# The order of TensorE's steps in a fused attention and feed-forward layer: from the first candidate in a priority, to the one with the earliest due time

## The reference

```python
qkv = x @ W_qkv.T
q, k, v = jnp.split(qkv, 3, axis=-1)
scores = jnp.einsum('bhqd,bhkd->bhqk', q, k) / math.sqrt(D_HEAD)
scores = jnp.where(mask, scores, -jnp.inf)
attn = jax.nn.softmax(scores, axis=-1)
out = jnp.einsum('bhqk,bhkd->bhqd', attn, v)
return out @ W_proj.T
...
x = _layernorm(x + _L0_attn_ref(x, L0_attn_W_qkv, L0_attn_W_proj), axis=-1)
x = _layernorm(x + _L0_ffn_ref(x, L0_ffn_w_gate, L0_ffn_w_up, L0_ffn_w_down), axis=-1)
```

## Time and profile before

| | |
|---|---|
| median of three runs | 1428.83 us (1426.91 to 1429.59) |
| profiled execution, its own time | 1426.97 us |
| its span, first to last instruction | 1425.3 us |
| busy: TensorE, VectorE, ScalarE, GpSimd | 95%, 78%, 62%, 24% of the span |
| mean granted TensorE clock | 0.984 of full |

### The profile page before, as it was taken

One profiled execution on the slowest core, in us unless ns is written; L12 is line 12 of the kernel. 1 busy time (PEld: TensorE's weight loads), 2 busy tenths in 40 slices (PEclk: granted clock), 3 DMA queues, 4 the chain that ended last, 5 costly groups with the idle time before them and its releaser, 6 DMA issues.

```text
span 1425.3 us, 29068 instructions
## 1 busy us (share of the span) xinstructions
PE 1353.2 (95%) x11348; PEld 661.3 (46%) x11348; DVE 1106.7 (78%) x1649; ACT 890.7 (62%) x1985; POOL 345.4 (24%) x448
## 2 busy tenths in 40 slices
PE   7999988999999999999999999999979999999997
PEld 4666643333333333333333333333336666666664
DVE  4455468988889888889888889888625877878876
ACT  2333335787787787787888788778763443444433
POOL 2000001212212212222122122121212543534434
PEclk9999977999999999999999999999999999999999
DMA  7555461221421212212212122121001122132111
GB/s 251 185 184 193 142 181 24 61 55 39 124 50 41 70 43 52 64 40 60 55 40 72 43 48 63 43 54 39 9 12 60 49 86 89 45 89 78 57 60 45
DMA packets 152313, 106.57 MB, mean 75 GB/s; under 512 B 79712, under 2 KB 139616, under 8 KB 152176
## 3 DMA queue, kind: packets, MB, share of 16 engines
q1 hardware_dynamic: 152176, 104.71, 25.8%
HBM read 62.13 MB, written 41.94 MB: 73 GB/s over the span
## 4 chain that ended last, share of the span: by engine, by line
PE 77%; DVE 10%; ACT 6%; issue 3%; POOL 1%; DMA 1%; SPq 0%; DVEq 0%; POOLq 0%; ACTq 0%
PE ps L1161 18%; PE ps L1146 12%; PE ps L1254 12%; DVE row_max L877 9%; PE ps L1080 8%; PE ps L1120 6%; PE ps L1269 5%; ACT probs L710 4%; PE ps L1201 4%; PE ps L1087 4%; PE ps L1173 3%; PE ps L1125 2%; PE ps L1239 1%; PE ps L1069 1%; ACT x_hi_rows L740 1%
## 5 line engine op out<-in xcount | busy, mean ns | idle before, releaser
L710 ACT ACTIVATE probs<-ps 128x512 f32<-128x512 f32 (+3 forms) x1536 | 641.3, 503 | 172.1 <-PE ps L1146 170.5
L877 DVE TENSOR_REDUCE row_max<-ps 128x2 f32<-128x1024 f32 (+1 forms) x512 | 569.2, 1153 | 41.4 <-PE ps L1125 20.0
L1146 PE MATMUL ps<-q_stack,k_stack 50*128 50x512 f16 (+3 forms) x1536 | 374.8, 331 | 20.1 <-ACT probs L710 13.2
L1161 PE MATMUL ps<-probs,v_ones 128*32 128x512 f32 (+3 forms) x3072 | 329.0, 500 | 4.0 <-POOL probs L617 2.7
L617 POOL TENSOR_SCALAR_AFFINE_SELECT probs<-probs 128x512 f32<-128x512 f32 x256 | 162.5, 635 | 675.7 <-ACT probs L710 673.9
L1120 PE MATMUL ps<-k_stack,q_stack 48*128 48x512 f16 (+3 forms) x1536 | 290.8, 334 | 9.0 <-DVE row_max L877 4.8
L1146 PEld LDWEIGHTS ps<-q_stack,k_stack 50*128 50x128 f16 x1536 | 109.3, 93 | 288.9 <-ACT probs L710 229.4
L639 POOL TENSOR_TENSOR h_lo<-h_sb,h_hi 128x512 f16<-128x512 f32 x96 | 119.3, 1249 | 197.1 <-ACT h_hi L759 197.1
L1125 PE MATMUL ps<-above,one_of_half 64*128 64x128 bf16 (+1 forms) x2048 | 154.5, 206 | 0.0
L1125 PEld LDWEIGHTS ps<-above,one_of_half 64*128 64x128 bf16 x2048 | 127.3, 97 | 35.0 <-issue 2.5
L751 ACT ACTIVATE silu<-ps 128x512 f32<-128x512 f32 x96 | 57.3, 597 | 135.4 <-PE ps L1254 135.4
(11 more groups left out here) (104 smaller groups left out, 1335.0 us busy)
## 6 DMA issues: line engine op xcount, KB each, us to landing
x_sb<-in_L_attn_x SPq DMA_DIRECT2D x32, 512.0 KB, 5.2
qk_parts<-parts SPq DMA_DIRECT2D x64, 256.0 KB, 2.2
q_stack<-qk_parts SPq DMA_DIRECT2D x192, 64.0 KB, 2.4
k_stack<-qk_parts SPq DMA_DIRECT2D x192, 64.0 KB, 2.4
v_rows<-v_sb SPq DMA_DIRECT2D x16, 512.0 KB, 3.0
v_flat<-v_rows SPq DMA_DIRECT2D x32, 256.0 KB, 3.2
attn_rows<-attn_sb SPq DMA_DIRECT2D x64, 128.0 KB, 2.1
v_sb<-attn_rows SPq DMA_DIRECT2D x16, 512.0 KB, 6.3
```

Source lines behind the costliest of these rows:

```text
L710: act.activation(probs[(NS * n + s) % RING][:, j, 0:w], ps[:, 4 + use % 3, 0:w], ACT.Exp, scale=scale_of_batch).then_inc(exp_done, 1)
L877: dve.tensor_reduce(row_max[:, half, :, p, qt], banks[:, :, 0:w], AX.X, ALU.max).then_inc(s_free, 1)
L1146: pe.matmul(ps[:, 4 + use % 3, 0:w * P], k_stack[n % NG][rows, p, tile_cols(kt)], q_stack[n % NG][rows, p, q0:q0 + w * P], start=True, sto ...
L1161: last = pe.matmul(ps[32 * j:32 * j + 32, 7, c0:c0 + w * P], v_ones[n % 2][:, kt, j, :], probs[(NS * n + s) % RING][:, j, 0:w * P], start= ...
```

## The change

Each candidate now gets a due time. A score is due `KEEP_ACT` (1000 ns) before ScalarE would run out of work, a maxima step `KEEP_DVE` (1000 ns) before VectorE would, with a large penalty once maxima are more than `LAG_MAX` (1.5) groups ahead of the values. A values step is due 600 ns after it could start, or 2400 ns before that when the ring of three slots is full; turns are due 500 ns before they could start. Twice the time that TensorE would stand waiting for a candidate is added, and the smallest sum is taken. `LEAD_ST` goes. The lengths in the model, the number of steps, their instructions, tiles and semaphores stay. The file grows by 13 lines, so every later line number shifts by 13.

```diff
@@ -46,7 +46,8 @@
     CAUSAL, ACT_POOL, POOL_PE = 594, 200, 100
     COPY, COPY_ROWS, SPLIT, NORMALISE = 478, 170, 800, 650
     ROWS_MOVED = 2700
-    LEAD_ST, LAG_MAX, GROUPS_AHEAD = 0.2, 1.5, 2
+    KEEP_ACT, KEEP_DVE, KEEP_PV, KEEP_TURN, FULL, WHOLE = 1000, 1000, 600, 500, 3000, 20000
+    LAG_MAX, GROUPS_AHEAD = 1.5, 2
     ns, nu, hg = len(slots), len(units), 4
     pe = act = dve = pool = o_free = 0
     half_free, bank, pair = [0, 0], [0, 0, 0], [0, 0]
@@ -56,17 +57,29 @@
     while pv < groups * ns or turns:
         could = []
         if turned in parts:
-            could.append((max(bank[banks % 3], parts[turned]), -9, "mT"))
+            could.append((max(bank[banks % 3], parts[turned]), "mT"))
         if turns:
-            could.append((max(turns[0][2], pair[pairs % 2]), -8, "oT"))
+            could.append((max(turns[0][2], pair[pairs % 2]), "oT"))
         if mx < groups * nu and mx // nu <= pv // ns + GROUPS_AHEAD:
-            could.append((pair[pairs % 2], mx / nu - LAG_MAX, "max"))
+            could.append((pair[pairs % 2], "max"))
         if st < groups * ns * hg and st // hg < pv + RING and st // hg // ns in rows:
-            could.append((max(bank[banks % 3], rows[st // hg // ns]), st / (ns * hg) - LEAD_ST, "st"))
+            could.append((max(bank[banks % 3], rows[st // hg // ns]), "st"))
         if pv in ready:
-            could.append((max(ready[pv], o_free if slots[pv % ns][1] == 0 else 0), pv / ns, "pv"))
-        now = [c for c in could if c[0] <= pe + 20] or [min(could)]
-        start, _, what = min(now, key=lambda c: c[1])
+            could.append((max(ready[pv], o_free if slots[pv % ns][1] == 0 else 0), "pv"))
+        best = None
+        for avail, kind in could:
+            if kind == "st":
+                due = max(avail, act - KEEP_ACT)
+            elif kind == "max":
+                due = max(avail, dve - KEEP_DVE) + max(0, mx / nu - pv / ns - LAG_MAX) * WHOLE
+            elif kind == "pv":
+                due = max(avail, pe) + (KEEP_PV if st // hg < pv + RING else KEEP_PV - FULL)
+            else:
+                due = avail - KEEP_TURN
+            late = due + 2 * (max(pe, avail) - pe)
+            if best is None or late < best[0]:
+                best = (late, max(pe, avail), kind)
+        _, start, what = best
         pe = max(pe, start)
         if what == "st":
             q, j = divmod(st, hg)
```

## The result

The changed kernel takes 1415.89 us (median of four runs, 1414.41 to 1418.63), the kernel before 1428.05 in the same comparison (four runs). The ratio is 0.9916, with a 95% interval of 0.9896 to 0.9937: faster by 12.2 us. The forecast of 1414 is 1.9 us low; the gain, forecast at 14.9 us, is 2.7 short, since the kernel before came out 0.8 faster here than in the runs that the forecast started from. The profiled execution took 1414.41 us.

The account below looks back on a forecast made before the run. No engine was taken as full: TensorE, VectorE and ScalarE starve each other by turns, with 3.7 of 26.03 us a group waiting. Order gain 18.4 less 3.5 for late landings is 14.9 us, giving 1414 us; range 1405 to 1422.

Parts of the forecast that it names:

- 18.4 was the term: Attention stage: the new order of unchanged steps saves 18.4 us by the layout, bounds 14 to 23.
- the place quoted for it: At 490.72 and 490.99 VectorE and ScalarE idle over a microsecond, because TensorE ran an output turn at 490.03.
- first three groups: Start of attention: old order takes 81.1 us, new 77.3, giving 3.8 us.
- groups 3 to 30: Steady attention: 27 times 0.47 us a group, 12.6 us gained.
- late landings: Max rows' DMAs: nine of 32 groups land late, costing 4.4 us together, charged 3.5, bounds 0 to 10.
- the end: End of attention: the new order gives 2.0 us.
- the twelve pieces: One group, from one values step to the next, slots 0 to 11: together 25.54, 25.52 before rounding.
- the slack: Maxima turn to next group's first score: score at 4.76 us, rows seen at about 4.5, leaving 0.27.
- Rival 1: Maxima transfer: ScalarE copies 0.35 later, groups grow 0.1, late landings count in full; 1421 us, chance 0.10.
- Rival 2: Maxima transfer takes the lead: copy 1.1 us late, chain 5.6, kernel slower at 1435 us; chance 0.04.
- Rival 3: TensorE's order: waits only change places, so no gain, 1429 us; chance 0.05.
- rival 4: Maxima matmuls on array halves held in program order: 20 us more gain, 1394 us; chance 0.03.

Follow-up runs that it names:

- e1: Changed kernel, order untouched, turned maxima rows stored by two DMAs instead of four; 1407.05 us, ratio to before 0.9854.
- e2: Kernel before the change, rows stored by two DMAs instead of four; 1426.07 us, ratio 0.998.
- e3: Changed kernel with KEEP_PV 0 instead of 600, so a values step is due as soon as it can start; 1479.13 us, ratio 1.0354.
- e8: Changed kernel with each maxima step's matmuls issued upper half first; 1415.0 us, ratio 0.9912.
- e5: Changed kernel with two DMAs for the rows and KEEP_ACT 1400, KEEP_PV 1000, KEEP_TURN 0; 1394.84 us, ratio 0.9763.
- e6: Changed kernel, four DMAs, ROWS_MOVED 3900, KEEP_ACT 3000, KEEP_DVE 1500, KEEP_PV 1000, LAG_MAX 1.75, waiting time counted three times; 1395.72 us, ratio 0.9764.

## Why the prediction was right, and where its terms were off

**The path.** That TensorE's order, with no step changed, moves the time held: the order alone is worth 19.0 us by e1 and e2 where 18.4 was the term. How much of the 0.43 us that a plain group gained is waits, and how much the array's own work (0.3 and 0.2 in the layout), no run separates. The waits that went are those named (a bank that ScalarE must empty, the output turn's wait for VectorE), as the table by line shows, though at the output turn the other engines' idle time moved rather than went: ScalarE of the changed kernel still waits 0.84 and VectorE 0.34 there, and 0.70 and 0.76 at the next steps, against 1.16 and 1.10 of the earlier trace rows. The timeline rows:

```profile
486.13 0.26 DVE L915 RECIPROCAL recip<-ps 128x16 f32<-128x16 f32 x1 [0.34 <-PE ps L1186]
...
488.21 4.62 DVE L890 TENSOR_REDUCE row_max<-ps 128x2 f32<-128x1024 f32 x4 [0.76 <-PE ps L1133]
...
486.34 1.21 ACT L723 ACTIVATE probs<-ps 128x256 f32<-128x256 f32 x4 [0.84 <-PE ps L1159]
488.25 3.56 ACT L723 ACTIVATE probs<-ps 128x128 f32<-128x128 f32 x9 [0.70 <-PE ps L1159]
```

So engines do starve each other by turns and the order moves it, but the place quoted for it is not where the gain was made.

**The terms.** The attention ends 12.8 us earlier in the trace.

| term | predicted | measured |
|---|---|---|
| before group 0's first values | 0 | 0.9 |
| first three groups, without a late landing | 3.8 | 3.6 |
| groups 3 to 30, without late landings | 12.6 | 10.5 (701.7 less 27 x 25.60) |
| the end | 2.0 | 3.1 |
| late landings | -3.5 | -5.4 |
| sum | 14.9 | 12.8 |

The lines are rounded. Two terms failed. The group was laid out at 25.52 and takes 25.60; the twelve pieces were each within 0.1, the largest misses in slots 3 (1.83 for 1.92) and 10 (1.25 for 1.18). Since 27 groups repeat it, 0.08 becomes 2.1 us. And the late landings were charged 3.5 out of 4.4 because "some is made up later"; none is. The nine late scores are together 5.3 us later than 4.77, and the nine spacings together 5.4 longer than 25.60. The late landings themselves were also later than the nine of before that the charge was made from (9.1 us in all against 6.4), so with the slack taken off, 5.4 came through. What the two ends gave on top, 0.9 and 1.1, had been put at nothing and at 2.0, and paid half of it back. That was luck. The 0.9 lies in stage A, which the change does not touch: its last projection matmul starts at 192.87 us in the trace of before and at 191.92 in that of after, and between 190.3 and 192.9 in the ten traces. And in the end of the old order the granted clock falls to 0.50 for 3.4 us, while that of the new order is through before its clock falls at 1056.2:

```profile
1037.53:1040.94 3.41, 3.41 (x17) 1.09 (x16) 0.69 (x1) 1.08 (x2) 0.63 (x1) 0.50 0.20 43
```

At half speed that is up to 1.7 us, an estimate. In the first three groups both sides were laid out short, 81.1 for 82.3 us and 77.3 for 78.7; only the difference held.

**The slack.** The first score was laid out 4.76 behind the turn and stands at 4.77; the copy was laid out 0.57 behind and is at 0.50. Plain rows land 4.37 behind the turn and a late score starts 0.05 behind its landing, so the slack is 0.35 and not 0.27; it swallowed two of the eleven late landings whole. Rival 1 asked for a copy 0.35 later and, by that, a spacing longer by 0.1 everywhere: the copy is not late, and the 0.08 that the spacing is longer are no work of the chain, since e1 leaves the plain groups as they were. What it said of the late landings, that they count in full, held for all that exceeded the slack. Rival 2 (1435) needed a chain over 5.27 in most groups; e3 shows its kind, each first score waiting for its rows, in an order that is less patient. Rival 3 fell with the result, rival 4 with e8.

**What should have shown.** The spacing equal in each group: right, at 25.60, but for the nine groups behind a late landing. No output turn behind VectorE: right but for 0.4 us in all. The score at 4.8, later only after a late landing: right. VectorE's and ScalarE's shares up by 2%: about half of it at most. Their instructions in the stretch rose by 0.9%, their busy times by 1.2% (698.54 for 690.11 us) and 0.2% (626.18 for 624.85), since the long groups bring the mean of groups 3 to 30 to 25.76, and the old one there was 25.99.

## What to carry to other kernels

Where an order is fixed ahead, lay out the new one with start-to-start distances from the trace and have it reproduce the old one first; here it gave the size of a gain of 1% to within a few microseconds, but the orders of e5 and e6, chosen by that layout, came out 5 to 10 us worse than it said. Look for the one transfer that the new order brings near its reader: its spread, not its median, is paid in full once the slack is under it, and shortening it (two DMAs for four, which also took most of the spread away) is worth much in one order and little in another. Look at the granted clock before a wait is priced: in e3 the long groups cost over twice what their rows were late. A planner's constants are knobs for the order they make, not lengths to be put right: one truer length took 8.5 us away, and six changed together, that length among them, gave 20.

## What was not expected of the hardware

Late landings of the four small DMAs come together with instruction packets of about 1 us each: the landing shown above took 3.1 us where 1.8 is usual. The time of the packet matters: in the traces of before and after, packets on q8 that start between 0.1 us ahead of the first issue and 0.3 behind it go with rows that are 0.07 to 0.61 us late, those that start over 2 us behind it with 0.87 to 1.48. Beside two DMAs no such packet goes with a late landing. The two move fewer packets, 60 less a group by the pages of after and e1 (152313 and 150393 in all). Whether that is the reason stays open, as does why the instruction packets come where they do. Storing the rows by two DMAs in place of four shortens the bare chain from 4.38 to 3.34 us, which is close to two issues of 0.59 fewer on SP's queue.
